# A three-stage attention and feed-forward block on one core: the order of TensorE's work in the first stage

## The chip, the cores and the metric

The kernel runs on one core of one Trainium2 chip. The metric is the device time of one execution in microseconds (us), smaller being better. The engines are named as in the profile: PE is TensorE's matmul, PEld its weight load, DVE VectorE, ACT ScalarE, POOL GpSimd, SP SyncE.

## What is computed

Sixteen sequences of 512 tokens with 256 features pass through four sublayers, each with a layer norm in front and a residual behind: attention A, a feed-forward network with weights rounded to -1, 0 and 1, attention B, and the same network again. Only attention A is touched by the change:

```python
Q = (X @ Wq).reshape(n, s, 16, 64)      # n = 16, s = 512; K and V likewise
raw_attn = einsum('bshe,bthe->bsth', Q, K / 8)
attn = softmax(raw_attn, axis=2)
A = einsum('bsth,bthe->bshe', attn, V).reshape(n, s, 1024)
P = gelu(A, approximate=False) @ Wpost
return X + P
```

## The kernel before, in words

**Stages.** The first stage is attention A of all sequences; it fills the first 2.17 ms. The rest is the second stage. All instructions of an engine are issued by one loop over slots (L450, L543, L747, L880, L1146), and the engines meet by semaphores only, so each engine works through its own list strictly in the order in which the loop issues it.

**Units and slots.** A unit is 128 query tokens of a pair of heads against all 512 keys: 4 units to a pair of heads, 32 to a sequence, 512 in all. Slot u is named after the unit whose exponentials are turned in it. `LEAD` is 4: in slot u the scores belong to units 4 ahead. Below, r is a slot's number within its sequence's 32.

**What one unit passes through.** PE makes scores (`a_scores`, L578, line L592) for two units at once, unit u in the first half of `ps_s` and unit u + 1 in the second, as matmuls on 64 rows of the array (two heads side by side). They wait until the exponentials of all units before are done, since there is one `ps_s`. DVE takes the row maximum (`a_unit_max`, L956), ACT the two exponentials with their sums (`a_exps`, L777), DVE the reciprocal (`a_invert`, L963), POOL multiplies (`a_normalise_exps`, L486). PE then turns the exponentials by eight 128x128 transposes (`a_transposes`, L605), four into each of two PSUM banks, and the two banks are copied to SBUF (`a_copy_turned`), the first by DVE (L970), the second by ACT (L784); in the slots r of `BOTH_TURNED` = (4, 20) both by DVE. For each two units PE multiplies with the values (`a_values`, L623), on 64 columns of the array. Every second two units DVE copies the result out (`a_copy_values`, L999).

**Fills.** Beside this PE makes the products of the coming and the last sequence: queries and keys ("qk", L216, then a high part by ACT at L803 and a low part by DVE at L981), values ("v", L223, copied by ACT or by DVE), the output product ("post", L658, added by DVE at L993) and the transposes of the normed input ("x", L640, high by ACT at L797, low by DVE at L977). The tables `XT`, `QK_SLOTS`, `VALUE_SLOTS` and `POST` (L240 to L242) say in which slot. There is about one a slot.

**Three banks.** The transposes' two fills for a unit and each product use one bank of three in turn (`bank`, L227). A fill waits until the fill three before it has been emptied:

```python
                        if fill >= 3:
                            wait_emptied(pe, fill - 3)
```

**Orders of the engines in a slot.** PE (L747): in an even slot u the scores of units u + 4 and u + 5, in an odd slot the values of two earlier units; then the transposes of unit u, then the slot's products. DVE (L1146): the maximum (first in odd slots, after the low parts in even ones), the reciprocal, the low parts and copies of the products of the slot before, the copy of the turned bank, then the copy of the values (every fourth slot), the casts of heads after the Gelu (`HEADS_HIGH`, L1005), and the pieces of the coming sequence's norm (`STATS` L925, `AGGREGATE` L942, `NORMALISE` L951). ACT (L880): the high parts of the products of the slot before, the exponentials, the copy of the turned bank, and at r = 19 and r = 35 (that is slot 3 of the next sequence) four Gelus (`GELUS`, L813). POOL and SP follow the same slots; SP loads a sequence's input at r = -22.

Of the kernel before, what the change touches and what calls it, by code (L numbers as in the profile page):

```python
# [13 lines left out]
def hybrid_block_kernel(nc, X, WQ, WK, WV, WPOST, WB, BQK, BV, WO, BO, W1T, B1, W2T, B2, COS, SIN, X1, OUT):  # L14
# [6 lines left out]
    BATCH, S, D = X.shape  # L21
# [18 lines left out]
    with ctx:  # L40
# [196 lines left out]
            ins.then_inc(bank_freed[fill % 3], 1)  # L237

        UNITS_ALL = BATCH * UNITS
        XT, QK_SLOTS = -9, (-7, -6)  # L240
        FIRST_VALUES, VALUE_SLOTS = (-5, -4, -1, 0), ((-8, -5, -4, -1), (7, 8, 15, 16))
        POST, LAST_POSTS = ((32, 32, 35, 36), (43, 44, 51, 52)), (45, 46, 47, 48)  # L242
        STATS, AGGREGATE, POWER, NORMALISE = (-16, -15), -14, -14, (-12, -11)
        RESIDUAL, LOAD_X, SAVE_X, LAST_SAVE = 13, -22, 54, 50
        GELUS, BOTH_TURNED = (19, 35), (4, 20)
        HEADS_HIGH, HEADS_LOW = ((21, 21, 22, 22), (37, 37, 38, 38)), ((22, 22, 23, 24), (38, 38, 39, 40))
# [2 lines left out]
        LAST_QK = ("qk", PAIRS - 1, 1, BATCH - 1)  # L249
        LOAD_W, LOAD_WB, LOAD_REST, SPLIT, ABS = 40, 484, 503, (508, 509), (471, 473)  # L250
        GAMMA, QUANTISE, SCALE, CLEAR = 474, (504, 506), 514, (513, 514)
        FIRST_CAST, FIRST_SPLIT, SPLIT_OF_PAIR = (None, None, -8, -5, -4, 5), (-11, -8, -7, -4, -2, 6), ((1, 2), (4, 5))
        SHIFT = 554

        def late(s, half):
# [68 lines left out]

        steps_of, fill_of, fills = {}, {}, 0
        for slot in range(FIRST_A, LAST + SHIFT):
            if 0 <= slot < UNITS_ALL:
                fill_of["turn", 0, slot], fill_of["turn", 1, slot] = fills, fills + 1
                fills += 2
            for todo in todo_of.get(slot, []):  # L330
                fill_of[todo] = fills
                fills += 1
            for step in (2 * (slot - SHIFT), 2 * (slot - SHIFT) + 1):
                for kind, part, i, s in at_of.get(step, []):
                    if kind in ("wo", "down", "v") and i % 2 == 1:
                        fill = fill_of[kind, part, i - 1, s]
                    else:
                        fill, fills = fills, fills + 1
                    fill_of[kind, part, i, s] = fill
                    steps_of.setdefault(step, []).append((kind, part, i, s, fill))  # L340
# [17 lines left out]
        with nc.Block() as block:  # L358
# [216 lines left out]
            def _(pe):  # L575
# [171 lines left out]
                for slot in range(FIRST_A, LAST + SHIFT):  # L747
                    if slot < LAST_A:
                        if slot % 2 == 0 and 0 <= slot + LEAD < UNITS_ALL:
                            a_scores(slot + LEAD)  # L750
                        if slot % 2 == 1 and 3 <= slot < UNITS_ALL:
                            a_values((slot - 3) // 2)
                        if slot == UNITS_ALL:
                            a_values(UNITS_ALL // 2 - 1)
                        if 0 <= slot < UNITS_ALL:
                            a_transposes(slot)
                        for todo in todo_of.get(slot, []):
                            a_product(todo)
                    u = slot - SHIFT
                    if 0 <= u < UNITS_ALL:  # L760
                        scores(u)
                    if 0 <= u - L < UNITS_ALL:
                        turned_scores(u - L)
                    if (u - L) % 2 == 0 and 0 <= (u - L) // 2 - 1 < UNITS_ALL // 2:
                        values((u - L) // 2 - 1)
                    for step in (2 * u, 2 * u + 1):
                        for todo in steps_of.get(step, []):
                            product(*todo)

            @block.scalar  # L770
            def _(act):
# [9 lines left out]
                def a_copy_turned(u):  # L781
                    fill = fill_of["turn", 1, u]
                    wait_filled(act, fill)
                    emptied(nc.scalar.activation(et_a[:, u % 4, 2:4, :, :].rearrange("p t h q -> p (t h q)"), bank(fill), ACT.Copy), fill)  # L784
# [94 lines left out]

                for slot in range(FIRST_A, LAST + SHIFT):  # L880
                    if slot < LAST_A:
                        for todo in todo_of.get(slot - 1, []):
                            a_high(todo)
                        if 0 <= slot + LEAD < UNITS_ALL:
                            a_exps(slot + LEAD)
                        if 0 <= slot < UNITS_ALL and slot % UNITS not in BOTH_TURNED:
                            a_copy_turned(slot)
                        for n in range(2, 6):
                            if slot == FIRST_CAST[n]:
                                cast_first_weights(n)  # L890
# [22 lines left out]
            def _(dve):  # L913
# [231 lines left out]

                for slot in range(FIRST_A, LAST + SHIFT):  # L1146
                    if slot < LAST_A:
                        if slot % 2 == 1 and 0 <= slot + LEAD < UNITS_ALL:
                            a_unit_max(slot + LEAD)
                        if 0 <= slot + LEAD - 2 < UNITS_ALL:  # L1150
                            a_invert(slot + LEAD - 2)
                        for todo in todo_of.get(slot - 1, []):
                            a_low(todo)
                        if slot % 2 == 0 and 0 <= slot + LEAD < UNITS_ALL:
                            a_unit_max(slot + LEAD)
                        if 0 <= slot < UNITS_ALL:
                            a_copy_turned(slot)
                        if slot % 4 == 2 and 6 <= slot < 4 * PAIRS * BATCH + 6:
                            a_copy_values((slot - 6) // 4)
                        for n in pairs_at(HEADS_HIGH, slot):  # L1160
                            a_heads_to_high(n)
                        for s in range(BATCH):
# [90 lines left out]
```

## Time and profile before

| | |
|---|---|
| time, median of 3 runs | 3924.65 us (3924.22 to 3927.91) |
| the profiled execution's own time | 3924.3 us |
| its span, first to last instruction | 3922.5 us |
| share of the span busy: PE, DVE, ACT, POOL | 95%, 70%, 59%, 49% |

The profile shows one execution. A line of a timeline is the start in us, the busy time in us, the engine, the line of the kernel, the operation, the tiles written and read, and how many instructions were merged into it; in square brackets stands the engine's idle time before it and what ended that. Times of PE's matmuls overlap, so they are read from start to start.

### The profile page before, as it was taken

How to read it: one execution, taken by the hardware profiler on the slowest of the kernel's cores; microseconds unless marked ns; L12 is line 12 of the kernel's file. 1: busy time of each engine (PE TensorE's matmuls, PEld its weight loads, DVE VectorE, ACT ScalarE, POOL GpSimd, SP SyncE). 2: the span in 40 equal slices, each digit the busy share in tenths (PEclk: the TensorE clock that was granted, in tenths of full speed). 3: DMA queues.
4: the chain of work that ended last, by engine and by line, in shares of the span. 5: the costliest groups of instructions: out<-in, count | busy, mean ns of one | idle time of the engine just before them, and what ended most of it. 6: DMA issues, size and time to landing. Idle time of an engine off the chain costs nothing.

```text
span 3922.5 us, 65128 instructions
## 1 busy us (share of the span) xinstructions
PE 3713.5 (95%) x24194; PEld 2506.1 (64%) x24194; DVE 2735.5 (70%) x4367; ACT 2320.5 (59%) x4501; POOL 1922.4 (49%) x1219
## 2 busy tenths in 40 slices
PE   8999999999999999999999678999999999999987
PEld 6777777777777777777777544555555555555534
DVE  6766667666766666676676657777777777777762
ACT  5666565565656665665666345666666666666654
POOL 4555555555555555555555443444444444444412
PEclk9999999999999999999999879999999999999988
DMA  2000000000000000000000033232232222233220
GB/s 76 7 12 12 1 12 12 1 12 12 12 1 12 12 7 6 12 12 1 12 15 21 21 51 55 54 54 53 54 55 53 54 54 53 54 55 55 50 44 17
DMA packets 90920, 114.19 MB, mean 29 GB/s; under 512 B 10800, under 2 KB 64432, under 8 KB 90608
## 3 DMA queue, kind: packets, MB, share of 16 engines
q1 hardware_dynamic: 90608, 110.02, 14.0%
q8 instruction: 197, 3.23, 0.3%
q14 instruction: 115, 0.94, 0.1%
HBM read 33.43 MB, written 25.17 MB: 15 GB/s over the span
## 4 chain that ended last, share of the span: by engine, by line
PE 76%; DVE 14%; ACT 4%; POOL 3%; issue 3%; DMA 0%; DVEq 0%; POOLq 0%; ACTq 0%
PE ps_o L623 11%; PE ps_s L592 10%; PE ps_t L605 8%; PE ps_t L216 7%; PE ps_o L699 5%; DVE max_b L1097 5%; PE ps_t L734 5%; PE ps_m L605 4%; PE ps_s L672 3%; PE ps_t L658 3%; PE ps_m L216 3%; PE ps_t L223 3%; PE ps_t L725 3%; PE ps_s L686 2%; PE ps_m L725 2%
## 5 line engine op out<-in xcount | busy, mean ns | idle before, releaser
L486 POOL TENSOR_TENSOR e_a<-e_a,recip 128x1024 f32<-128x1024 f32 x512 | 969.4, 1894 | 959.7 <-DVE recip L963 959.6
L777 ACT ACTIVATE e_a<-ps_s,neg_max 128x512 f32<-128x512 f32 x1024 | 694.2, 684 | 553.7 <-DVE neg_max L956 553.3
L1097 DVE TENSOR_REDUCE max_b<-ps_s 128x2 f32<-128x1024 f32 x512 | 623.3, 1218 | 227.8 <-PE ps_s L672 226.3
L819 ACT ACTIVATE et<-ps_s 128x1024 f32<-128x1024 f32 x512 | 523.2, 1022 | 396.8 <-PE ps_s L686 396.8
L956 DVE TENSOR_REDUCE neg_max<-ps_s 128x2 f32<-128x1024 f32 x512 | 623.2, 1217 | 70.3 <-PE ps_s L592 70.3
L623 PE MATMUL ps_o<-et_a,v_a 128*64 128x256 f32 x4096 | 501.4, 387 | 6.3 <-DVE heads_a L999 1.4
L592 PE MATMUL ps_s<-raw_a 64*128 64x512 f32 x3072 | 426.8, 410 | 11.4 <-ACT e_a L777 11.3
L522 POOL TENSOR_TENSOR h_lo<-h,h_hi 128x512 fp32r<-128x512 f32 x256 | 327.0, 1293 | 166.7 <-ACT h_hi L863 166.7
L605 PE MATMUL ps_t<-ident,e_a 128*128 128x128 f32 x2660 | 395.0, 281 | 8.1 <-DVE xl L1140 5.5
L623 PEld LDWEIGHTS ps_o<-et_a,v_a 128*64 128x64 f32 x4096 | 280.0, 137 | 190.6 <-issue 77.0
L970 DVE COPY et_a<-ps_t 128x512 f32<-128x512 f32 x366 | 251.1, 688 | 204.3 <-PE ps_t L605 200.1
L605 PEld LDWEIGHTS ps_t<-ident,e_a 128*128 128x128 f32 x2660 | 290.5, 141 | 139.4 <-issue 129.7
L592 PEld LDWEIGHTS ps_s<-raw_a 64*128 64x128 f32 x3072 | 271.3, 185 | 135.1 <-issue 73.3
L672 PE MATMUL ps_s<-k_stack,q_stack 48*128 48x512 f32 x1024 | 262.2, 508 | 93.0 <-DVE max_b L1097 92.6
L510 POOL TENSOR_TENSOR rstd<-rstd,minus_half 128x4 f32<-128x4 f32 x48 | 49.3, 1027 | 513.1 <-DVE rstd L1068 513.0
L699 PE MATMUL ps_o<-et,v_b 128*32 128x512 f32 x2048 | 283.3, 626 | 0.0
L672 PEld LDWEIGHTS ps_s<-k_stack,q_stack 48*128 48x128 f32 x1024 | 99.5, 188 | 258.7 <-issue 140.1
L784 ACT ACTIVATE et_a<-ps_t 128x512 f32<-128x512 f32 x299 | 178.2, 596 | 118.0 <-PE ps_t L605 118.0
L734 PE MATMUL ps_t<-w,h_hi 128*128 128x256 f32 x752 | 204.0, 306 | 25.9 <-POOL h_lo L522 25.7
L605 PE MATMUL ps_m<-ident,e_a 128*128 128x128 f32 x1436 | 225.1, 279 | 0.0
L686 PE MATMUL ps_s<-q_stack,k_stack 50*128 50x512 f32 x1024 | 214.3, 410 | 9.7 <-ACT et L819 8.6
L981 DVE SCALAR_TENSOR_TENSOR raw_a<-ps_t,raw_a 128x512 fp32r<-128x512 f32 x181 | 124.4, 687 | 130.0 <-ACT raw_a L803 125.0
(197 smaller groups left out, 7432.5 us busy)
## 6 DMA issues: line engine op xcount, KB each, us to landing
q_stack<-roped_q SPq DMA_DIRECT2D x256, 64.0 KB
k_stack<-roped_k SPq DMA_DIRECT2D x256, 64.0 KB
x_a<-X SPq DMA_DIRECT2D x16, 512.0 KB, 3.8
X<-x_a SPq DMA_DIRECT2D x16, 512.0 KB, 2.9
x_ahead<-X SPq DMA_DIRECT2D x16, 512.0 KB, 3.8
X<-x_ahead SPq DMA_DIRECT2D x16, 512.0 KB, 4.3
q_stack<-roped_q SPq DMA_DIRECT2D x256, 32.0 KB
k_stack<-roped_k SPq DMA_DIRECT2D x256, 32.0 KB
```

Of the source, the lines that this page charges most:

```text
L216: last = nc.tensor.matmul(out, w[:, k, c0:c0 + P], xs[:, k, :], start=(i == 0), stop=(i == len(todo) - 1))
L486: nc.gpsimd.tensor_tensor(e_a[:, u % 5, :, :], e_a[:, u % 5, :, :], factor, ALU.mult).then_inc(e_normed, 1)
L592: last = mm(ps_s[:, 2 * j + h, :], raw[rows, q_part, c:c + P], raw[rows, k_part, :], start=(m == 0), stop=(m == 2))
L605: last = nc.tensor.transpose(bank(fill)[:, c:c + P], e_a[:, u % 5, j, t * P:(t + 1) * P], ident[:, :])
L623: last = mm(out, v_a[:, t, c:c + HA], et_a[:, 2 * (q % 2):2 * (q % 2) + 2, t, h, :], start=(t == 0), stop=(t == TB - 1))
L672: last = mm(ps_s[:, score_bank(u) + h, :], q_stack[rows, pair, block_ * P:(block_ + 1) * P], k_stack[rows, pair, :], start=True, stop=True)
L699: last = mm(ps_o[32 * h:32 * (h + 1), :], v_b[:, s % 2, keys, 4 * quad + h, :], et[:, (2 * w + h // 2) % 5, h % 2, :], start=(keys == 0), ...
L734: last = mm(half, hidden[:, f, tokens], w2[:, f, :], start=(f == 0 and m == 0), stop=(f == FT - 1 and m == 1))
L777: ins = nc.scalar.activation(e_a[:, u % 5, h, :], ps_s[:, 2 * (u % 2) + h, :], ACT.Exp, bias=neg_max[:, u % 5, h:h + 1], accum_out=sums[:, ...
L819: nc.scalar.activation(et[:, v % 5, :, :], ps_s[:, 2:4, :], ACT.Exp)\
L956: nc.vector.reduce_max(neg_max[:, u % 5, :], ps_s[:, 2 * (u % 2):2 * (u % 2) + 2, :], AX.X, negate=True)\
L1097: nc.vector.reduce_max(max_b[:, u // 4 % 2, :, u % 4], ps_s[:, score_bank(u):score_bank(u) + 2, :], AX.X, negate=True).then_inc(max_done, 1)
```

## The change

PE's order is laid out anew in groups of two slots. In an even slot PE makes the scores (as before), then the transposes of both units, then the products of both slots, then the values of these same two units, which before came in a later odd slot. The bank numbers follow: four fills of transposes, then the products. ACT makes the high parts of two slots' products together at the head of an even slot, and in each slot copies the turned bank ahead of the exponentials. DVE makes the low parts of two slots together at the head of an even slot, then in each slot maximum, reciprocal, copy of the turned bank, and the copy of the values comes two slots earlier, in slots divisible by 4. The tables of the products, of the norm and of the first weights are moved two slots earlier; `GELUS`, `BOTH_TURNED`, `HEADS_HIGH`, `HEADS_LOW`, `RESIDUAL`, `LOAD_X` and `SAVE_X` stay as they are.

```diff
-        XT, QK_SLOTS = -9, (-7, -6)
-        FIRST_VALUES, VALUE_SLOTS = (-5, -4, -1, 0), ((-8, -5, -4, -1), (7, 8, 15, 16))
-        POST, LAST_POSTS = ((32, 32, 35, 36), (43, 44, 51, 52)), (45, 46, 47, 48)
-        STATS, AGGREGATE, POWER, NORMALISE = (-16, -15), -14, -14, (-12, -11)
+        XT, QK_SLOTS = -11, (-9, -8)
+        FIRST_VALUES, VALUE_SLOTS = (-7, -6, -3, -2), ((-10, -7, -6, -3), (5, 6, 13, 14))
+        POST, LAST_POSTS = ((30, 30, 33, 34), (41, 42, 49, 50)), (45, 46, 47, 48)
+        STATS, AGGREGATE, POWER, NORMALISE = (-18, -17), -16, -16, (-14, -13)
...
-            if 0 <= slot < UNITS_ALL:
-                fill_of["turn", 0, slot], fill_of["turn", 1, slot] = fills, fills + 1
-                fills += 2
-            for todo in todo_of.get(slot, []):
-                fill_of[todo] = fills
-                fills += 1
+            if slot % 2 == 0:
+                for u in (slot, slot + 1):
+                    if 0 <= u < UNITS_ALL:
+                        fill_of["turn", 0, u], fill_of["turn", 1, u] = fills, fills + 1
+                        fills += 2
+                for u in (slot, slot + 1):
+                    for todo in todo_of.get(u, []):
+                        fill_of[todo] = fills
+                        fills += 1
...
                         if slot % 2 == 0 and 0 <= slot + LEAD < UNITS_ALL:
                             a_scores(slot + LEAD)
-                        if slot % 2 == 1 and 3 <= slot < UNITS_ALL:
-                            a_values((slot - 3) // 2)
-                        if slot == UNITS_ALL:
-                            a_values(UNITS_ALL // 2 - 1)
-                        if 0 <= slot < UNITS_ALL:
-                            a_transposes(slot)
-                        for todo in todo_of.get(slot, []):
-                            a_product(todo)
+                        if slot % 2 == 0:
+                            for u in (slot, slot + 1):
+                                if 0 <= u < UNITS_ALL:
+                                    a_transposes(u)
+                            for u in (slot, slot + 1):
+                                for todo in todo_of.get(u, []):
+                                    a_product(todo)
+                            if 0 <= slot < UNITS_ALL:
+                                a_values(slot // 2)
...
-                        for todo in todo_of.get(slot - 1, []):
-                            a_high(todo)
+                        if slot % 2 == 0:
+                            for u in (slot - 2, slot - 1):
+                                for todo in todo_of.get(u, []):
+                                    a_high(todo)
+                        if 0 <= slot < UNITS_ALL and slot % UNITS not in BOTH_TURNED:
+                            a_copy_turned(slot)
                         if 0 <= slot + LEAD < UNITS_ALL:
                             a_exps(slot + LEAD)
-                        if 0 <= slot < UNITS_ALL and slot % UNITS not in BOTH_TURNED:
-                            a_copy_turned(slot)
...
-                        if slot % 2 == 1 and 0 <= slot + LEAD < UNITS_ALL:
+                        if slot % 2 == 0:
+                            for u in (slot - 2, slot - 1):
+                                for todo in todo_of.get(u, []):
+                                    a_low(todo)
+                        if 0 <= slot + LEAD < UNITS_ALL:
                             a_unit_max(slot + LEAD)
                         if 0 <= slot + LEAD - 2 < UNITS_ALL:
                             a_invert(slot + LEAD - 2)
-                        for todo in todo_of.get(slot - 1, []):
-                            a_low(todo)
-                        if slot % 2 == 0 and 0 <= slot + LEAD < UNITS_ALL:
-                            a_unit_max(slot + LEAD)
                         if 0 <= slot < UNITS_ALL:
                             a_copy_turned(slot)
-                        if slot % 4 == 2 and 6 <= slot < 4 * PAIRS * BATCH + 6:
-                            a_copy_values((slot - 6) // 4)
+                        if slot % 4 == 0 and 4 <= slot < 4 * PAIRS * BATCH + 4:
+                            a_copy_values((slot - 4) // 4)
```

## Rows read from the trace of the kernel before

**Rows 1.** Stretches: us; busy PE, PEld, DVE, ACT, POOL; granted clock; DMA share; GB/s.

```profile
42.97:2060.00 2017.03, 2005.12 (x14172) 1467.39 (x14171) 1378.04 (x2360) 1226.37 (x2855) 1100.32 (x626) 1.00 0.03 9
...
27.46:30.90 3.44, 3.44 (x10) 2.72 (x9) 3.44 (x4) 1.92 (x5) 0.00 (x0) 0.53 0.00 0
```

**Rows 2.** PE's largest wait from 120 to 2050 us: us in total, times, longest.

```profile
PE ps_t L640 <- DVE raw_a L981: 3.3, 10, 0.3
```

**Rows 3.** Timeline of PE, two slots of the first stage and the same place 16 pairs on.

```profile
1005.13 1.66 PE L592 MATMUL ps_s<-raw_a 64*128 64x512 f32 x12
1006.72 0.66 PE L605 MATMUL ps_m<-ident,e_a 128*128 128x128 f32 x4
1007.22 0.60 PE L605 MATMUL ps_t<-ident,e_a 128*128 128x128 f32 x4
1007.57 0.47 PE L223 MATMUL ps_t<-wa_hi,xh_a 128*128 128x512 f32 x1
1007.89 0.39 PE L223 MATMUL ps_t<-wa_lo,xh_a 128*128 128x512 f32 x1
1008.12 0.40 PE L223 MATMUL ps_t<-wa_hi,xh_a 128*128 128x512 f32 x1
...
1009.13 1.95 PE L623 MATMUL ps_o<-et_a,v_a 128*64 128x256 f32 x16
1011.01 0.66 PE L605 MATMUL ps_m<-ident,e_a 128*128 128x128 f32 x4
...
1013.44 1.66 PE L592 MATMUL ps_s<-raw_a 64*128 64x512 f32 x12
...
1140.26 1.66 PE L592 MATMUL ps_s<-raw_a 64*128 64x512 f32 x12
```

**Rows 4.** The chain that ended last: four transposes behind others, start and us.

```profile
1007.38 0.44 PE ps_t L605 x4
```

**Rows 5.** Timeline of DVE in the same two slots.

```profile
1006.14 1.23 DVE L956 TENSOR_REDUCE neg_max<-ps_s 128x2 f32<-128x1024 f32 x1 [0.21 <-PE ps_s L592]
1007.42 0.69 DVE L970 COPY et_a<-ps_m 128x512 f32<-128x512 f32 x1
1008.02 1.22 DVE L956 TENSOR_REDUCE neg_max<-ps_s 128x2 f32<-128x1024 f32 x1
1009.15 0.16 DVE L963 RECIPROCAL recip<-sums 128x2 f32<-128x2 f32 x1
```

**Rows 6.** Timelines of PE and DVE near the start: waits of PE.

```profile
25.83 1.70 PE L592 MATMUL ps_s<-raw_a 64*128 64x512 f32 x12 [1.94 <-ACT e_a L777]
...
54.86 0.69 DVE L981 SCALAR_TENSOR_TENSOR raw_a<-ps_t,raw_a 128x512 fp32r<-128x512 f32 x1 [3.04 <-ACT raw_a L803]
...
55.60 0.50 PE L216 MATMUL ps_t<-xh_a,wa_hi 128*128 128x512 f32 x1 [0.16 <-DVE raw_a L981]
```

**Rows 7.** Timeline of DVE: the pieces that come in some slots only.

```profile
1000.49 1.10 DVE L1005 CAST heads_parts<-heads_a 128x512 fp32r<-128x512 f32 x2
...
1045.61 0.74 DVE L925 BATCH_NORM_STATS2 stats<-x_a 128x6 f32<-128x256 f32 x2
...
1049.81 0.68 DVE L999 COPY heads_a<-ps_o 128x512 f32<-128x512 f32 x1
1050.40 0.37 DVE L942 BATCH_NORM_AGGREGATE mean_var<-stats 128x2 f32<-128x6 f32 x4
...
1058.72 0.73 DVE L951 TENSOR_SCALAR xn_a<-x_a,mean_var,rstd 128x256 f32<-128x256 f32 x2
```

**Rows 8.** Timeline of ACT: exponentials, a copy, table load and Gelus.

```profile
1024.03 0.69 ACT L777 ACTIVATE e_a<-ps_s,neg_max 128x512 f32<-128x512 f32 x1 [2.98 <-DVE neg_max L956]
...
1025.37 0.60 ACT L784 ACTIVATE et_a<-ps_t 128x512 f32<-128x512 f32 x1
...
1054.53 1.28 ACT L813 ACT_TABLE_LOAD   x1
1055.83 2.19 ACT L813 ACTIVATE heads_a<-heads_a 128x512 f32<-128x512 f32 x4
```

More of the change, by code:

```diff
@@ L251, in hybrid_block_kernel @@
         GAMMA, QUANTISE, SCALE, CLEAR = 474, (504, 506), 514, (513, 514)
-        FIRST_CAST, FIRST_SPLIT, SPLIT_OF_PAIR = (None, None, -8, -5, -4, 5), (-11, -8, -7, -4, -2, 6), ((1, 2), (4, 5))
+        FIRST_CAST, FIRST_SPLIT, SPLIT_OF_PAIR = (None, None, -10, -7, -6, 3), (-13, -10, -9, -6, -4, 4), ((1, 2), (4, 5))
         SHIFT = 554
```

## The prediction

> **What bounds the kernel now.** I read the stretches first. In the first stage PE is busy 2005 of 2017 us at a granted clock of 1.00, the level of 2.4 GHz, while DVE is busy 1378 us, ACT 1226 and POOL 1100 [rows 1]. The waits agree: between 120 and 2050 us the largest that PE has is 3.3 us in total [rows 2]. So PE's own work sets the stage, and a busy PE still holds unproductive time, which the timeline shows. Two slots, here called a pair, last 8.31 us from scores to scores (1005.13 to 1013.44). Within them the starts are: scores 0, transposes 1.59, product 2.44, values 4.00, transposes 5.88, then a second product. Matmuls of one product follow each other every 0.23 us (1007.89, 1008.12), but from product to values the step is larger: six matmuls take 1.56, not 1.38 [rows 3]. Four transposes behind others need 0.44 us [rows 4], behind scores 0.50 [rows 3]. Whenever PE goes over between full products, scores on 64 rows and values on 64 columns, it loses 0.15 to 0.2 us. A sequence is 16 pairs and lasts 1140.26 - 1005.13 = 135.1 us [rows 3]; extra fills and waits make it 2.1 more than 16 x 8.31.
>
> **What the change does to PE alone.** A pair becomes scores, both units' transposes, two products, values: three goings-over instead of four. By starts [rows 3, 4]: scores 1.59; the first unit's transposes 0.50 + 0.44; the second's 0.44 + 0.35 to the product's start; first product 0.32 + 5 x 0.23 = 1.47; second, up to the values, 5 x 0.23 + 0.33 = 1.48; values 1.88, as from values to transposes now (from values to scores no row exists: I bound it by 0.1 either way, half of what a going-over costs, and take none). Sum 8.15, against 8.31: 0.16 less, and over 256 pairs 41 us.
>
> **The new waits.** The banks decide whether PE gets that. Number a pair's fills 0 to 3 (the first unit's banks 0 and 1, the second's 2 and 3), then products 4 and 5. Fill 3 needs fill 0 emptied, 4 needs 1, 5 needs 2. DVE empties 0 and 2, ACT 1 and 3. A bank released by DVE lets PE go on 0.05 us later: the low part ends at 54.86 + 0.69 = 55.55, the product starts at 55.60 [rows 6].
>
> DVE's list in a pair is: two low parts, maximum, reciprocal, copy of fill 0, even-slot extras E, maximum, reciprocal, copy of fill 2. The first maximum can't start before half of the scores are made, 1.01 us after they start. The next instruction starts 1.13 us after a maximum, some 0.08 after a reciprocal, 0.60 after a copy, and a copy lasts 0.69 [rows 5]. Fill 0 is full in time for a copy at 2.29 (1007.42 - 1005.13), so:
> - fill 0 is empty at 2.98, and fill 3 starts at 3.03 where PE alone would have 2.97 [rows 3 to 6]. Restarting costs some 0.05 more, so fill 4 starts at 3.44 and fill 5 could at 4.91.
> - the second maximum starts at 2.89 + E, the copy of fill 2 at 4.10 + E, fill 2 is empty at 4.79 + E and fill 5 may start at 4.84 + E.
>
> **With E = 0** fill 5 starts at 4.91 and the pair lasts 4.91 + 1.48 + 1.88 = 8.27: the gain is nearly eaten already. **With E above 0.07** PE stands still in front of the second product, which then costs 1.56 up to the values, and the pair lasts 8.28 + E. That is the core of my forecast: the copy of fill 2 is behind DVE's even-slot extras, which in the kernel before no bank waited for so closely.
>
> **The extras**, by the step to the next instruction, 0.08 less than the merged length [rows 7]: copy of values 0.60 (1049.81 to 1050.40), two casts 1.02, statistics 0.66, aggregation 0.40, normalisation 0.65. Their odd-slot halves come after the copy of fill 2 and meet a DVE that is idle until the next low parts, so I cost them nothing; that cover is about 2 us.
>
> **The Gelus.** ACT's list in a pair is: high parts, copy of fill 1, exponentials, copy of fill 3, exponentials. It copies fill 1 at 2.73 (0.64 after its first transpose at 2.09), ready at 3.33, just before fill 4 at 3.44. With exponentials 1.34 and copies 0.60 [rows 8] it ends at 3.33 + 1.34 + 0.60 + 1.34 = 6.61; the next scores wait for that but come at 8.2 and later, so nothing is lost. High parts and low parts of the two products follow and are done about when the next pair begins. Not so behind the Gelus. They stay at r = 19 and 3, while the products moved: formerly the high parts at the head of the slot after were absent (those slots held "post" products), now there is one of a key product from slots 19 and 3. Table load 1.28 and Gelus 2.19 [rows 8] end at 10.08 after that pair's start. Then the high part (0.60, as a copy), then DVE's low part (0.60 to the next), and only then the first maximum:
> - r = 4: the pair before lasts 8.27, so the high part starts at 1.81 and the maximum at 3.01. From it to the end of the copy of fill 2 are 1.20 + 0.60 + 1.20 + 0.69 = 3.69, and E = 1.20 (copy of values, and the second bank, which is DVE's here). PE goes on at 7.95; 1.56 + 1.88 give 11.39.
> - r = 20: the pair before lasts 8.93, the maximum starts at 2.35, PE goes on at 7.29. Two "x" fills take 0.05 + 0.88, going over 0.10, values 1.88: 10.20.
>
> **The sum for a sequence:** four pairs without extras (r = 2, 10, 26, 30) 33.1, a third fill at r = 30 1.4; copy of values at r = 0, 8, 12, 24, 28: 5 x 8.88 = 44.4; casts at r = 6, 22: 2 x 9.30 = 18.6; r = 14 8.94; r = 16 (copy and aggregation) 9.28; r = 18 8.93; r = 4 11.39; r = 20 10.20. Together 146.2 against 135.1: 11.1 more, over 16 sequences 178. The first sequence has no Gelus before r = 4, nor casts at r = 6, and the last prepares no other: 5 less. Sum +173.
>
> What else moves: SP's load of a sequence at r = -22 is now four slots ahead of its statistics instead of six, some 17 us, for a transfer that the page shows landing in 3.8; no DMA is added. POOL multiplies unit u + 2 after its reciprocal at about 2.2 and unit u + 3 after 4.0 + E, 1.9 us each, both before the next pair's transposes. POOL's rows for the heads' low parts at r = 8 end near 5.5, where the "post" product of that pair would start anyway. The first sequence's ramp is worth a few us either way; I take none.
>
> The profiled execution took 3924.3 us, 0.35 below the median. 3924.3 + 173 = 4097, or 4098 by the median.
>
> **The rivals.**
> *PE gets its gain* (chance 0.08): the copies of fill 2 are in time everywhere. For it speaks that the stage is PE's alone now [rows 1, 2]; against it that E must stay under 0.07 while it is 0.4 or more in 12 of 16 pairs. Time 3924 - 41 = 3883. The point from which it decides is E = 0.07.
> The Trainium skill, "TensorEngine Tiling (Array Packing)", Key Properties, says that changing the tiling mode drains TensorE; by that rule alone one drain a pair fewer is a gain, and the time would be this rival's. The steps between kinds in rows 3 agree with it; it says nothing of the banks.
>
> *The waits just eat the gain* (0.03): every pair is like those without extras, 8.27, within 0.2% of before. The extras speak against it.
>
> *No pile-up behind the Gelus* (0.13): the high part is hidden, and r = 4 and r = 20 cost only their E of 1.20, that is 9.48 and 8.95 (the two "x" fills take 0.53 less than a product). 3.2 less a sequence, 50 in all: 4048. Against it stands ACT's order.
>
> *The clock falls in the pairs behind the Gelus* (0.14): At r = 4 PE stands still for some 3 us in parts (fill 3 starts at 4.95 instead of 2.97, fill 5 at 7.95). Near the start it stood 1.94 us in front of the scores at 25.83 [rows 6], and from 27.46 to 30.90 the granted clock was 0.53 [rows 1], nearly the level of 1.2 GHz, which lost 3.44 x 0.47 = 1.6 us. 31 such pairs cost 50: 4148. Against it: much of the slow work would lie under DVE's chain.
>
> *My forecast* has 0.62. All but the first two are slower. About 0.2% (8 us) is what a measurement of this kernel can tell from no change: faster 0.08, same 0.03, slower 0.89. **The range**: 4048 and 4148 at the other cases, each widened by part of the 26 us (256 x 0.1) that the unseen going-over from values to scores may take or give: 4035 to 4175; outside lie the first two rivals and a little more.
>
> **What would show it.** In the changed profile PE has waits of some 0.6 us for DVE's turned bank (L970) at the second product in most pairs, absent before; pairs alternate between about 8.3 and 8.9 us; r = 4 and r = 20 last over 10; DVE's and ACT's busy times stay. If PE waits nowhere and a sequence lasts 132.5 us, the bank argument is wrong; if scores come much later than 1.9 us after values begin, the price of going over is.

## The result and the profile after

The changed kernel takes 4220.4 us (median of four runs, 4219.05 to 4221.73). The kernel before, run beside it on the same chip, takes 3925.3 (four runs). The ratio is 1.0747, 95% interval 1.0731 to 1.0763. The forecast was slower by 173 us; it is slower by 295, and the time lies outside the range.

First three lines of the page after: span, busy times, and the chain that ended last by engine.

```profile
span 4217.3 us, 65129 instructions
PE 3792.7 (90%) x24194; PEld 2520.5 (60%) x24194; DVE 2850.9 (68%) x4367; ACT 2294.0 (54%) x4501; POOL 1933.4 (46%) x1219
...
PE 53%; DVE 24%; issue 11%; ACT 7%; POOL 4%; DVEq 0%; DMA 0%; POOLq 0%; ACTq 0%
```

PE was busy 95% of a span of 3922.5 and is now busy 90% of 4217.3. DVE's share of the chain is 24%. Where PE stands is in its waits from 120 to 2100 us, the largest first (us in total, times, longest):

```profile
PE ps_t L216 <- DVE et_a L976: 62.2, 34, 2.8
PE ps_m L216 <- DVE et_a L976: 32.3, 17, 2.8
PE ps_t L608 <- DVE et_a L976: 15.6, 17, 1.1
PE ps_t L223 <- DVE et_a L976: 15.1, 34, 0.7
PE ps_t L661 <- DVE et_a L976: 11.6, 17, 1.1
```

Where [rows 2] had 3.3 us as the largest, all of the large ones are now waits for DVE's copy of a turned bank (L976, before L970). Most stand at a product (L216, L223, L661), as forecast; but those at L216, the products of queries and keys, reach 2.8 us where the forecast had some 0.6 for most waits.

A stretch of the first stage in the columns of [rows 1]:

```profile
120.00:2100.00 1980.00, 1798.99 (x12291) 1282.08 (x12286) 1283.88 (x2042) 1038.81 (x2469) 962.28 (x545) 0.99 0.02 7
```

In these 1980 us PE stands idle for 181; in the 2017 us of [rows 1] it was 12.

An ordinary pair with the copy of the values (r = 0), timeline of PE and DVE; compare [rows 3] and [rows 5]:

```profile
1100.70 1.65 PE L595 MATMUL ps_s<-raw_a 64*128 64x512 f32 x12
1102.98 0.69 DVE L976 COPY et_a<-ps_t 128x512 f32<-128x512 f32 x1
1103.59 0.68 DVE L1005 COPY heads_a<-ps_o 128x512 f32<-128x512 f32 x1
1104.19 1.21 DVE L962 TENSOR_REDUCE neg_max<-ps_s 128x2 f32<-128x1024 f32 x1
1105.39 0.67 DVE L976 COPY et_a<-ps_t 128x512 f32<-128x512 f32 x1
1106.11 0.39 PE L661 MATMUL ps_t<-wpost_hi,heads_parts 128*128 128x256 f32 x1 [0.34 <-DVE et_a L976]
1107.74 1.95 PE L626 MATMUL ps_o<-et_a,v_a 128*64 128x256 f32 x16
1109.62 1.67 PE L595 MATMUL ps_s<-raw_a 64*128 64x512 f32 x12
```

This is the forecast's chain as it was drawn. The copy of fill 0 starts 2.28 after the scores (forecast 2.29), then the copy of the values, the second maximum, and the copy of fill 2, which ends at 5.36; the second product starts at 5.41, and the pair lasts 8.92 (forecast 8.88).

The timeline of a pair r = 22, which holds the casts of heads; with r = 6 it is the worst:

```profile
1052.01 1.65 PE L595 MATMUL ps_s<-raw_a 64*128 64x512 f32 x12
1054.29 0.69 DVE L976 COPY et_a<-ps_t 128x512 f32<-128x512 f32 x1
1054.39 1.90 POOL L489 TENSOR_TENSOR e_a<-e_a,recip 128x1024 f32<-128x1024 f32 x1 [3.95 <-DVE recip L969]
1054.89 1.67 DVE L1011 CAST heads_parts<-heads_a 128x512 fp32r<-128x512 f32 x1
1056.24 1.46 POOL L493 TENSOR_TENSOR heads_parts<-heads_a,heads_parts 128x512 fp32r<-128x512 f32 x1
1056.49 1.50 DVE L1011 CAST heads_parts<-heads_a 128x512 fp32r<-128x512 f32 x1
1057.91 1.21 DVE L962 TENSOR_REDUCE neg_max<-ps_s 128x2 f32<-128x1024 f32 x1
1059.11 0.66 DVE L976 COPY et_a<-ps_m 128x512 f32<-128x512 f32 x1
1059.83 0.50 PE L216 MATMUL ps_m<-xh_a,wa_hi 128*128 128x512 f32 x1 [2.75 <-DVE et_a L976]
1061.46 3.54 PE L626 MATMUL ps_o<-et_a,v_a 128*64 128x256 f32 x16
1064.93 1.65 PE L595 MATMUL ps_s<-raw_a 64*128 64x512 f32 x12
```

Two casts took 1.10 in [rows 7]; here they take 3.09 (1054.89 to 1057.98), the first beside POOL's multiplication (to 1056.29), the second beside POOL's next work (to 1057.70). Each ends 0.28 us behind that instruction of POOL. PE stands still 2.75 us in front of the second product, and then the values take 3.47 from start to start instead of 1.88. The stretch of that time shows why (columns as in [rows 1]):

```profile
1061.40:1064.95 3.55, 3.55 (x19) 1.74 (x18) 0.69 (x1) 0.60 (x1) 0.99 (x1) 0.53 0.02 5
```

The granted clock is 0.53, near the level of 1.2 GHz. Not every such pair meets this. In r = 22 of another sequence PE waits as long at the same place, and in the values behind it the clock is 1.00:

```profile
294.43 0.50 PE L216 MATMUL ps_t<-xh_a,wa_hi 128*128 128x512 f32 x1 [2.75 <-DVE et_a L976]
```

```profile
296.04:297.92 1.88, 1.88 (x19) 1.06 (x18) 0.69 (x1) 0.60 (x1) 0.97 (x1) 1.00 0.00 0
```

The pairs by r, each the median over the sequences, in us from scores to scores, worked out from the starts in the traces; the pairs not listed lie within 0.06 of the forecast:

| r | before | forecast | after | after less forecast |
|---|---|---|---|---|
| 4 | 8.34 | 11.39 | 11.18 | -0.21 |
| 6 | 8.31 | 9.30 | 11.30 | +2.00 |
| 8 | 8.31 | 8.88 | 9.13 | +0.25 |
| 16 | 8.31 | 9.28 | 9.64 | +0.36 |
| 18 | 8.51 | 8.93 | 10.08 | +1.15 |
| 20 | 8.34 | 10.20 | 9.74 | -0.46 |
| 22 | 8.50 | 9.30 | 12.89 | +3.59 |
| 30 | 8.31 | 9.67 | 9.76 | +0.09 |
| all 16 | 135.1 | 146.2 | 153.1 | +6.9 |

A median hides that r = 6 and r = 22 have two lengths. In all 30 of these pairs that hold casts, the last sequence's r = 22 apart, PE waits 2.73 to 2.76 us at L216. In 15 the clock holds, and they last 11.3 us, r = 6 and r = 22 alike; in the other 15 it falls, and they last 12.6 to 14.2 (r = 6, 6 of 15 sequences) or 12.7 to 12.9 (r = 22, 9 of 15).

From its first scores to its last the stage takes 2432.5 us instead of 2146.7, 286 more, where the forecast had 173. The first scores start at 21.72 instead of 19.27, from the first stage's last scores to the second stage's first there are 122.0 us instead of 117.0, and the rest of the second stage takes 1.5 more. So of the 122 us that the forecast missed, 113 lie in the pairs and 9 at the edges.

**The duration that grew.** DVE's groups by line over 120 to 2100 us, first of the kernel before, then of the changed one (count, busy us, mean ns, idle before):

```profile
L1005 DVE CAST heads_parts<-heads_a 128x512 fp32r<-128x512 f32 x118 | 65.7, 597 | 0.0
L951 DVE TENSOR_SCALAR xn_a<-x_a,mean_var,rstd 128x256 f32<-128x256 f32 x56 | 20.3, 405 | 0.0
```

```profile
L962 DVE TENSOR_REDUCE neg_max<-ps_s 128x2 f32<-128x1024 f32 x414 | 504.3, 1218 | 292.2 <-PE ps_s L595 292.2
L1011 DVE CAST heads_parts<-heads_a 128x512 fp32r<-128x512 f32 x104 | 134.5, 1333 | 0.0
L957 DVE TENSOR_SCALAR xn_a<-x_a,mean_var,rstd 128x256 f32<-128x256 f32 x49 | 45.9, 976 | 0.0
```

A cast grew from 597 ns on average to 1333, the normalisation of a block from 405 to 976. The maximum, which reads PSUM, kept its 1218. Sorted by whether POOL was running an instruction when the DVE instruction ran (median us of one, in brackets how many, from 120 to 2300 us of both traces):

| | before, POOL idle | before, POOL busy | after, POOL idle | after, POOL busy |
|---|---|---|---|---|
| cast of heads | 0.416 (78) | 0.771 (48) | 0.414 (29) | 1.668 (87) |
| normalisation | 0.404 (56) | none | 0.402 (28) | 1.574 (28) |

With POOL idle nothing changed. Beside POOL both take about 1.2 us longer. They aren't slower by a fixed amount: every cast over 0.45 us, 46 of them before and 93 after, ends 0.28 to 0.29 us behind the end of a POOL instruction, and every such normalisation 0.15. So each has waited for POOL to finish, and what it costs is what is left of POOL's instruction. The new order puts three casts of four beside it: the reciprocal is now ahead of the casts in DVE's list, and it is what POOL's multiplication waits for.

### The profile page after: what moved, and what is told of

The parts are those of the page before. It is cut to its first block, busy times and chain, and to the rows that moved or that the text cites. A ratio compares the mean times of both kernels' runs of the same rounds, so it can differ in the third digit from the quotient of the medians.

```text
span 4217.3 us, 65129 instructions
## 1 busy us (share of the span) xinstructions
PE 3792.7 (90%) x24194; PEld 2520.5 (60%) x24194; DVE 2850.9 (68%) x4367; ACT 2294.0 (54%) x4501; POOL 1933.4 (46%) x1219
## 4 chain that ended last, share of the span: by engine, by line
PE 53%; DVE 24%; issue 11%; ACT 7%; POOL 4%; DVEq 0%; DMA 0%; POOLq 0%; ACTq 0%
PE ps_o L626 10%; PE ps_s L595 6%; DVE neg_max L962 5%; PE ps_o L702 4%; DVE max_b L1103 4%; PE ps_t L737 4%; PE ps_t L216 4%; PE ps_s L675 3%; DVE et_a L976 3%; PE ps_t L661 2%; PE ps_t L728 2%; PE ps_t L223 2%; PE ps_m L216 2%; PE ps_t L608 2%; DVE heads_parts L1011 2%
## 5 line engine op out<-in xcount | busy, mean ns | idle before, releaser
L788 ACT ACTIVATE et_a<-ps_t 128x512 f32<-128x512 f32 x330 | 198.4, 601 | 643.8 <-PE ps_t L608 643.8
L626 PE MATMUL ps_o<-et_a,v_a 128*64 128x256 f32 x4096 | 520.4, 398 | 25.8 <-DVE et_a L976 24.1
L608 PEld LDWEIGHTS ps_t<-ident,e_a 128*128 128x128 f32 x2764 | 300.6, 141 | 125.9 <-issue 72.9
L987 DVE SCALAR_TENSOR_TENSOR raw_a<-ps_t,raw_a 128x512 fp32r<-128x512 f32 x166 | 114.5, 690 | 291.1 <-ACT raw_a L807 291.1
L788 ACT ACTIVATE et_a<-ps_m 128x512 f32<-128x512 f32 x150 | 90.1, 601 | 318.3 <-PE ps_m L608 318.3
L976 DVE COPY et_a<-ps_t 128x512 f32<-128x512 f32 x361 | 244.3, 680 | 1.3 <-PE ps_t L608 1.3
```

The source lines that it names most:

```text
L608: last = nc.tensor.transpose(bank(fill)[:, c:c + P], e_a[:, u % 5, j, t * P:(t + 1) * P], ident[:, :])
L626: last = mm(out, v_a[:, t, c:c + HA], et_a[:, 2 * (q % 2):2 * (q % 2) + 2, t, h, :], start=(t == 0), stop=(t == TB - 1))
L976: emptied(nc.vector.tensor_copy(out, bank(fill)), fill)
```

## The experiments

Each edit is made to the changed kernel. The theory is the forecast's, that DVE's even-slot extras lie ahead of the copy that the second product waits for, and, formed after the result, that the casts and normalisations among them grow beside POOL; the rivals are named in the expectations.

**e1: the reciprocal behind the extras, in even slots.** POOL's multiplication then starts after the casts, and nothing else of DVE's list moves.

```diff
-                        if 0 <= slot + LEAD - 2 < UNITS_ALL:
+                        if slot % 2 == 1 and 0 <= slot + LEAD - 2 < UNITS_ALL:
                             a_invert(slot + LEAD - 2)
...
                                 a_normalise(s, 2 * NORMALISE.index(r))
+                        if slot % 2 == 0 and 0 <= slot + LEAD - 2 < UNITS_ALL:
+                            a_invert(slot + LEAD - 2)
```

> One edit to the changed kernel: in even slots DVE's reciprocal comes after all extras instead of ahead of the copy of the turned bank, so POOL's multiplication of that unit can't start before the casts and the normalisation are done; nothing is left out. Theory (DVE's casts and normalisation, SBUF to SBUF, stand behind a running POOL multiplication: 1.67 us a cast and 1.57 us a normalisation where POOL is busy, 0.41 and 0.40 where it is idle): casts in slot r = 22 drop to 0.42 us, the pairs r = 6 and r = 22 from 11.30 and 12.89 to about 9.05, r = 18 from 10.08 to 8.95, r = 16 from 9.64 to 9.3; a sequence from 153.1 to about 145.5 us and the whole to about 4103 us. Rival (the casts are slow by what they wait for or by themselves, whatever POOL does): within 8 us of 4220.

Measured: 4152.2 us, ratio to the kernel before 1.0568 [1.0550, 1.0586]; 68 us less than the changed kernel, where the rival says none. The timeline of DVE and POOL in r = 22:

```profile
1025.34 0.74 DVE L1011 CAST heads_parts<-heads_a 128x512 fp32r<-128x512 f32 x2
1026.00 0.15 DVE L969 RECIPROCAL recip<-sums 128x2 f32<-128x2 f32 x1
1026.23 1.89 POOL L489 TENSOR_TENSOR e_a<-e_a,recip 128x1024 f32<-128x1024 f32 x1 [4.63 <-DVE recip L969]
```

The same two casts take 0.74 instead of 3.09. The pairs with casts and normalisations come down as expected: r = 6 from 11.30 to 9.01, r = 22 from 12.89 to 9.13, r = 18 from 10.08 to 9.00. So the durations were POOL's doing, through the reciprocal's place. Of the 117 us that I expected, 49 are missing, and 33 of these are r = 8, which rose from 9.13 to 10.45 in 7 sequences and to 12.0 in 8. There POOL, started later, finishes the heads' low parts later, which the output product reads; PE waits 1.90 to 1.91 us for them in all 15, and behind 8 of these waits the clock falls. PE's wait in r = 8 of such a sequence, then the stretch behind it:

```profile
962.63 0.36 PE L661 MATMUL ps_t<-wpost_hi,heads_parts 128*128 128x256 f32 x1 [1.90 <-POOL heads_parts L493]
```

```profile
963.00:967.70 4.70, 4.70 (x29) 3.07 (x28) 0.75 (x2) 0.00 (x0) 1.33 (x1) 0.64 0.00 0
```

**e2: both products of a pair of one kind, in an even slot.** This takes the key product's high part away from between the Gelus and the exponentials.

```diff
-        XT, QK_SLOTS = -11, (-9, -8)
-        FIRST_VALUES, VALUE_SLOTS = (-7, -6, -3, -2), ((-10, -7, -6, -3), (5, 6, 13, 14))
-        POST, LAST_POSTS = ((30, 30, 33, 34), (41, 42, 49, 50)), (45, 46, 47, 48)
+        XT, QK_SLOTS = -11, (-8, -8)
+        FIRST_VALUES, VALUE_SLOTS = (-6, -6, -2, -2), ((-10, -10, -6, -6), (6, 6, 14, 14))
+        POST, LAST_POSTS = ((30, 30, 34, 34), (42, 42, 50, 50)), (45, 46, 47, 48)
```

> Only the tables of the products are edited in the changed kernel: both products of a pair of heads in one pair of slots (r = 0, 4, ..., 20, 24, 28), values and output products two by two in the others, so that the pairs with the Gelus hold no product with a high part on ACT. Theory (behind the Gelus the high part of the key product delays DVE's low part and with it the first maximum): r = 4 falls from 11.18 to about 9.5; r = 20, which now holds four fills, stays near 10; a sequence loses some 2.5 us, and the whole comes to about 4180 us. Rival (the Gelus' own delay of the exponentials sets those pairs): r = 4 stays over 11, the whole within 8 us of 4220.

Measured: 4200.5 us, ratio 1.0687 [1.0671, 1.0703]. The pair r = 4 lasts 9.48 instead of 11.18; r = 20, which now makes four fills, 11.09 instead of 9.74. ACT and DVE at r = 4, whose scores start at 958.30:

```profile
957.74 2.19 ACT L817 ACTIVATE heads_a<-heads_a 128x512 f32<-128x512 f32 x4
959.32 1.22 DVE L962 TENSOR_REDUCE neg_max<-ps_s 128x2 f32<-128x1024 f32 x1 [2.37 <-PE ps_s L595]
959.95 1.28 ACT L781 ACT_TABLE_LOAD   x1
```

The maximum starts 1.02 after the scores, not 2.80 as in the changed kernel (967.60 after 964.80). The pile-up behind the Gelus is real, it is what the forecast said, and it is small: 2 us a sequence.

**e3: all of DVE's extras into odd slots,** where they come behind the copy of fill 2.

```diff
-        STATS, AGGREGATE, POWER, NORMALISE = (-18, -17), -16, -16, (-14, -13)
+        STATS, AGGREGATE, POWER, NORMALISE = (-21, -19), -17, -17, (-15, -13)
-        HEADS_HIGH, HEADS_LOW = ((21, 21, 22, 22), (37, 37, 38, 38)), ((22, 22, 23, 24), (38, 38, 39, 40))
+        HEADS_HIGH, HEADS_LOW = ((21, 21, 23, 23), (37, 37, 39, 39)), ((22, 22, 24, 24), (38, 38, 40, 40))
...
-                        if slot % 4 == 0 and 4 <= slot < 4 * PAIRS * BATCH + 4:
-                            a_copy_values((slot - 4) // 4)
+                        if slot % 4 == 1 and 5 <= slot < 4 * PAIRS * BATCH + 5:
+                            a_copy_values((slot - 5) // 4)
```

> DVE's extras alone are moved from even slots to odd ones, behind the copy of fill 2: copy of the values in slots 1, 5, 9, ..., casts at r = 21, 21, 23, 23 and 5, 5, 7, 7 (POOL's low parts at 22, 22, 24, 24), statistics at -21, -19, aggregation and power at -17, normalisation at -15, -13. Theory (PE waits at the second product for the copy of fill 2, which stands behind the extras): pairs without Gelus fall to 8.3, r = 8 rises to 10 because its output product waits for POOL's low parts; a sequence falls by about 14 us, the whole to about 3996 us. Rival (the pairs are bound by something else of the new order, as the exponentials on ACT): less than a third of that, above 4150 us.

Measured: 4030.5 us, ratio 1.0259 [1.0244, 1.0274]: 190 us less from places alone. Pairs with extras now last 8.28 to 8.32 (r = 0, 6, 12, 14, 16, 18, 22), the forecast's 8.27 for E = 0. Yet DVE's groups (120 to 2100 us) are still far slower than in the kernel before (597 and 405 ns):

```profile
L1011 DVE CAST heads_parts<-heads_a 128x512 fp32r<-128x512 f32 x114 | 114.9, 1047 | 0.0
L957 DVE TENSOR_SCALAR xn_a<-x_a,mean_var,rstd 128x256 f32<-128x256 f32 x56 | 46.0, 861 | 0.0
```

A slow cast costs nothing there. What it costs is decided by its place ahead of the copy of fill 2; how much, by POOL. r = 4 (10.57), r = 8 (10.36, and 11.9 to 12.0 in 4 sequences; PE waits 1.8 us for the heads' low parts) and r = 20 (10.01) stayed long, and the whole is 34 us above the 3996 expected.

**e4: in odd slots the copy of the turned bank ahead of the maximum.** The extras stay where the change put them.

```diff
+                        if slot % 2 == 1 and 0 <= slot < UNITS_ALL:
+                            a_copy_turned(slot)
                         if 0 <= slot + LEAD < UNITS_ALL:
                             a_unit_max(slot + LEAD)
...
-                        if 0 <= slot < UNITS_ALL:
+                        if slot % 2 == 0 and 0 <= slot < UNITS_ALL:
                             a_copy_turned(slot)
```

> One edit to the changed kernel: in odd slots DVE copies fill 2 ahead of the second maximum instead of behind it. Theory: fill 2 is then empty at about 3.6 us + E instead of 4.79 + E, so PE doesn't wait for it as long as E is under 1.28 us: the pairs with the copy of the values, the statistics and the aggregation fall to 8.3, those with casts and normalisation lose 1.2 us each, r = 4 and r = 20 about 1.2 each; a sequence falls to about 142 us, the whole to about 4045 us. Rival (the later second maximum makes the exponentials, and through them the next scores, late): the gain is given back, above 4150 us, with PE waiting at the scores for ACT.

Measured: 4082.9 us, ratio 1.0392 [1.0376, 1.0407]. DVE in a pair with the copy of the values:

```profile
1098.42 0.68 DVE L1005 COPY heads_a<-ps_o 128x512 f32<-128x512 f32 x1
1099.02 0.68 DVE L976 COPY et_a<-ps_t 128x512 f32<-128x512 f32 x1
1099.62 1.21 DVE L962 TENSOR_REDUCE neg_max<-ps_s 128x2 f32<-128x1024 f32 x1
```

The maximum no longer stands between, and the pair lasts 8.23. r = 6 and 22, with 3 us of casts still ahead of the copy, last 10.1 (r = 22 11.1 in 5 sequences): one maximum less (1.21) than 11.3, and the clock no longer falls in them (the last sequence's r = 22 apart), where PE's wait at the second product is now 1.56 in most. I expected 4045; r = 20 accounts for the difference. It was to fall by 1.2 and rose from 9.74 to 10.6 in 5 sequences and to between 11.7 and 12.2 in 9, 25 us in all. There PE waits at fills 2 and 3 for the "x" low part and the copy behind it, and in those 9 the clock goes down:

```profile
988.88 0.63 PE L608 MATMUL ps_t<-ident,e_a 128*128 128x128 f32 x4 [1.25 <-DVE raw_a L987]
990.58 1.11 PE L608 MATMUL ps_m<-ident,e_a 128*128 128x128 f32 x4 [1.07 <-DVE et_a L976]
```

```profile
989.00:992.00 3.00, 1.93 (x10) 1.60 (x10) 3.00 (x6) 2.03 (x6) 1.89 (x1) 0.71 0.60 183
```

**e5, e6, e7: the remedies together.** e6 is e2 + e3. e7 is e2 + e3 + e4. e5 is e7 with the copy of the values left in even slots.

> The changed kernel with all causes found taken away at once: products paired as in e2, copy of fill 2 first as in e4, casts and the norm's pieces in odd slots as in e3 (the copy of the values stays in even slots). Theory (nothing else binds, and one going-over a pair less is worth 0.1 us or less since fill 3 still waits for the copy of fill 0): pairs of 8.25 us, r = 20 with four fills 9.3, a sequence 133 us, the whole about 3900 us, faster than before by 0.6%. Rival (the new order of PE costs in itself): pairs of 8.4 us or more, the whole above 3950 us.

> As e5, but without the copy of fill 2 first, and with the copy of the values in odd slots too. Theory: with E = 0 in all pairs fill 2 is empty at 4.79 us, in time for fill 5, so the pairs last 8.28, r = 20 9.3; a sequence 133.5 us, the whole about 3908 us. Rival (the copy of fill 2 binds even with no extras): pairs over 8.4 us, the whole above 3940 us.

> As e5, with the copy of the values in odd slots too, behind the second maximum. Theory: E is 0 in all pairs and fill 2 is empty at 3.6 us everywhere; the pairs are those of e5 within 0.02 us, the whole within 6 us of e5. Rival (the later copy of the values delays the values product that waits for it): r = 4, 12, 20, 28 longer than e5's, the whole over 10 us above e5.

Measured, ratios to the kernel before: e5 3955.4 us, 1.0067 [1.0054, 1.0081]; e6 3950.5, 1.0058 [1.0046, 1.0071]; e7 3942.1, 1.0037 [1.0025, 1.0050]. All ordinary pairs are as expected, 8.28 in e6 and 8.23 in e5 and e7. My totals for e5 and e6 were still 55 and 42 us too low, and e7 is 13 below e5 where I expected at most 6. The pair behind the Gelus, expected at 9.3, is 42 of the 55 and 18 of the 42. r = 20 lasts 11.45 in e5, or 12.6 to 13.1 in 7 sequences in which the clock falls behind PE's wait of 1.85; 10.49 in e6 and 11.09 in e7. The difference between e5 and e7 is this pair's too. In e6 r = 4 (8.89) and the edges (9 us more than in the kernel before) hold most of the rest. r = 20 makes four fills, two of them "x", behind ACT's late high parts. PE's wait at an "x" fill in e7:

```profile
1071.49 0.65 PE L643 MATMUL ps_t<-ident,xn_a 128*128 128x128 f32 x4 [1.49 <-DVE raw_a L987]
```

**e8 and e9: the two "x" fills apart,** in two pairs, once one pair earlier and once one later. Both build on e7. e8 needs the norm earlier too, and so overwrites the normed input that the last key products still read: it does not compute the block, and its time stands for the order alone.

```diff
-        XT, QK_SLOTS = -11, (-8, -8)
+        XT, QK_SLOTS = (-13, -11), (-8, -8)
-        STATS, AGGREGATE, POWER, NORMALISE = (-21, -19), -17, -17, (-15, -13)
+        STATS, AGGREGATE, POWER, NORMALISE = (-23, -21), -19, -19, (-17, -15)
-        FIRST_A, LAST_A, LATE = -21, UNITS_ALL + 20, 4
+        FIRST_A, LAST_A, LATE = -23, UNITS_ALL + 20, 4
```

> As e7, with the two transposes of the normed input in two pairs (r = 19 and 21 instead of both at 21) and the norm's pieces two slots earlier for it (statistics -23, -21, aggregation and power -19, normalisation -17, -15; the loops begin at slot -23). Theory (in e7 the second of them, fourth fill behind two key products, waits for the low part of the first, which DVE does in the next slot: r = 20 at 11.09): r = 18 and r = 20 come to about 8.8, the others stay at 8.23 to 8.35, a sequence 133.5 us; the whole about 3912 us, under the kernel before. Rival (r = 20 is long by the norm or by the clock, not by that bank): r = 20 stays over 10, the whole at 3935 to 3945 us.

Measured: 3936.5 us, 1.0024 [1.0014, 1.0034]: the rival's time, not mine. r = 18 is 8.79 as expected, but r = 20 stays at 10.10. The rival's reason, the norm or the clock, is not what the trace shows: the norm's pieces aren't in that pair, and the clock stays at 1.00. One "x" high part still stands behind the Gelus, its low part and then the first maximum follow, and PE waits at fill 3 for the copy of fill 0 behind them:

```profile
1062.01 1.21 DVE L962 TENSOR_REDUCE neg_max<-ps_s 128x2 f32<-128x1024 f32 x1
1063.94 0.66 PE L608 MATMUL ps_t<-ident,e_a 128*128 128x128 f32 x4 [1.07 <-DVE et_a L976]
```

That pair's scores start at 1059.71, so the maximum comes 2.30 behind them.

e9 moves the second "x" later, and the values' products with it:

```diff
-        XT, QK_SLOTS = -11, (-8, -8)
-        FIRST_VALUES, VALUE_SLOTS = (-6, -6, -2, -2), ((-10, -10, -6, -6), (6, 6, 14, 14))
+        XT, QK_SLOTS = (-11, -9), (-8, -8)
+        FIRST_VALUES, VALUE_SLOTS = (-6, -6, -2, -2), ((-6, -6, -4, -2), (6, 6, 14, 14))
```

> As e7, with the two transposes of the normed input at r = 21 and 23 (pairs 20 and 22), and the first values' products of the next sequence at r = 26, 26, 28, 30 for it, so that no pair has over three fills; the norm stays as in e7, and nothing is overwritten early, which e8 does: there the first transpose's high part replaces the input that the last key products still read, so its output differs. Theory (a fourth fill needs the first product's bank, which DVE empties only in the next slot, and a high part in pair 18 would stand behind the Gelus again): r = 20 falls from 11.09 to about 8.8, r = 22 to some 7.5, r = 28 and r = 30 rise to 9.7; a sequence 133.3 us, the whole about 3908 us, under the kernel before. Rival (r = 20 is long by DVE's casts and copies or by the clock): r = 20 stays over 10, the whole over 3930 us.

Measured: 3942.9 us, 1.0040 [1.0026, 1.0053]; missed again. Inside the stage it did what it should: r = 20 lasts 8.90, and the largest wait of PE from 120 to 2100 us, then the same engine's work in a stretch of a sequence, are:

```profile
PE ps_o L626 <- ACT et_a L788: 17.5, 15, 1.2
```

```profile
1000.00:1135.00 135.00, 133.83 (x954) 99.63 (x952) 100.76 (x160) 79.45 (x193) 74.70 (x43) 1.00 0.03 9
```

PE is busy 133.8 of 135 us, and a sequence between the first and the last lasts 134.9 against 135.1 before. That is all that the order is worth: 0.3 us a sequence, some 4 in all, less than was lost elsewhere. From its first scores to its last the stage takes 2150.9 us against 2146.7, since the first sequence lasts 133.7 instead of 126.8. The first scores start at 24.6 instead of 19.27, from the last scores to the second stage there are 121.5 us instead of 117.0, and the second stage takes about 3 more. No kernel that was run beats the kernel before.

## Why the prediction came out as it did

- **The chain through the banks: right.** Fill 5 waits for DVE's copy of fill 2, which stands behind the extras and the second maximum. Pairs with the copy of the values last 8.87 to 8.91 (forecast 8.88; only r = 8, with 9.13, was longer: there the output product waits 0.6 us for POOL's low parts of the heads, until 5.66 behind the scores, where the forecast had "near 5.5" and no cost), r = 14 lasts 8.94 (8.94), pairs without extras 8.28 to 8.32 (8.27). e3 and e4 take the cause away from two sides, and both bring the pair back to 8.28 or 8.23.
- **"The extras, by the step to the next instruction ... two casts 1.02 ... normalisation 0.65": this step failed.** In the changed order they take 3.09 (r = 6 and 22) and 1.86 (r = 18). I took durations from the kernel before as if they belonged to the instruction; they belong to the instruction and to what POOL does beside it. The kernel before held the warning: 48 of its 126 casts took 0.771 instead of 0.416 beside POOL, and the 1.10 of [rows 7] is one of 0.77 and one of 0.41. I had worked out when POOL's two multiplications would run ("at about 2.2"), and that the casts would start at about 2.9, and did not lay one over the other. Misses of 2.00 at r = 6, of 2.00 without the clock at r = 22, and 1.15 at r = 18 are these durations; another 0.24 of r = 16's 0.36 is the small operation on the variances (0.41 instead of 0.17). That is 5.4 of the 6.9 us, about 80 of the 122 that the forecast missed; the clock, below, is 25. The range missed the time for the same reason: it held bounds for the unseen step from values to scores, but none for durations that had a row.
 The Trainium skill has this rule, in "SBUF — State Buffer", section "Who interferes with whom": DVE and GpSimd share a pair of SBUF ports as an exclusive lock, and a copy, cast or tensor_scalar in a two-port mode takes it for the whole instruction or waits for whoever holds it, while an instruction with at most one SBUF input outside those modes does not contend. The traces agree: casts and tensor_scalar from SBUF went from 0.41 and 0.40 to 1.67 and 1.57 beside a POOL instruction of 1.90 and ended a fixed 0.28 and 0.15 behind POOL's, and the copies from PSUM stayed at 0.68 in the same place.
- **"DVE's and ACT's busy times stay": wrong for DVE,** for the same reason; the two groups above alone grew from 86 us to 180, with fewer instructions in the window.
- **The clock: right mechanism, wrong pair.** I gave it a chance of 0.14, in the pairs behind the Gelus. At r = 4 PE stands for some 2 us in parts, and the granted clock stays 1.00 from 964.8 to 976. At r = 6 and r = 22 it stands for 2.75 at once, and behind 15 of these 30 waits the clock falls, to 0.53 in the stretch above. That costs 1.6 us in most of them (values 3.54 instead of 1.95), the price of [rows 1], and 25 in all. Behind the other 15, as long, it holds: what decides is not shown.
- **The Gelus: right, a little too dear.** 11.18 instead of 11.39 and 9.74 instead of 10.20; the first maximum came at 2.80 after the scores instead of 3.01. e2 showed that the key product's high part causes it.
- **The saving on PE alone: half of it was seen.** The forecast had 8.15 for PE without waits. The shortest ordinary pairs of any run are 8.23 (e4, e5, e7, e8, e9), against 8.31. The bounded step from values to scores is 1.88, as taken (1050.13 to 1052.01 in the changed kernel). The remaining 0.08 a pair arises at fill 3, as the forecast had it. In a pair of 8.23 of e9 the scores start at 1005.01, DVE's copy of fill 0 runs from 1007.28 to 1007.97, fill 3 starts at 1008.03, 3.02 behind the scores, and the first product 3.44 behind them; the forecast had 3.03 and 3.44, with "some 0.05" for the restart, which no row of the kernel before showed and which is 0.06 here (0.41 from fill 3 to the product instead of 0.35), and 3.32 for that product without the wait. The rest of the pair is 0.04 shorter than summed. No run moved that copy.
- **The edges: costed at nothing, cost 9 us:** 2.5 at the start, 5 between the stages, 1.5 in the second stage. What it would take to get these back was not tried.
- **The rival that PE gets its gain** (3883) fell at the point named, E = 0.07. The rule of "TensorEngine Tiling (Array Packing)", Key Properties of the Trainium skill that stood beside it holds as far as the traces go: with the waits gone, one going-over fewer saves 0.08 a pair. It decides nothing while a bank is late.

## What to carry to other kernels

A duration from the profile belongs to its surroundings: before an SBUF-to-SBUF cast or tensor_scalar of DVE is moved, or the instruction that releases POOL, lay the two engines' new timelines over each other. When a product must wait for one particular copy, everything ahead of that copy in its engine's list is on the path, and everything behind it is nearly free: e3 took 190 us off with casts that still took 1047 ns on average. With an order written out by hand, a small saving for each step must also pay for the edges, the start and the hand-over to the next stage, which here took more than the steady state gave. And where a pair's length has two values, a median of it hides the second.

## What the runs showed of the hardware that was not expected

- The size of the interference: in the changed kernel a DVE cast of 128x512 from SBUF took 0.41 us alone and up to 1.755 beside POOL; the normalisation of 128x256 0.40 and up to 1.62. Those that met POOL ended 0.28 and 0.15 us behind its instruction. Each cast of a couple can meet another POOL instruction, so that two took 3.09.
- A wait of 2.75 us of PE in one piece was followed by a granted clock of 0.53 (1061.40 to 1064.95), one of 1.90 by 0.64 (e1, 963.0 to 967.7), and waits of 1.25 and 1.07 shortly behind each other by 0.71 (e4, 989 to 992). None of the three always was: the first kind in 15 of 30 pairs, the second in 8 of 15, the third in 9 of 14. Several shorter waits at r = 4, 2 us in sum, were followed by none in 15 sequences. So a stall of some two microseconds may cost another 1.6 behind itself, and its length alone does not tell.
